# Attention tower: the softmax sums' reciprocals taken on 128 partitions, with two DMAs, in place of 64 partitions in slices

## The reference

```python
h = h + attn0(layernorm(h))      # 8 heads of 8 features, 1024 x 1024 scores, a window bias
h = h + ffn0(layernorm(h))       # two routed layers of 128, relu
h = h + attn1(layernorm(h))      # 8 heads of 8 features, no bias
h = h + ffn1(layernorm(h))       # 8 experts of 128, gelu, top 2
```

```python
attn = softmax(q @ k.T * 8 ** -0.5 (+ bias))   # over the last axis
out  = (attn @ v) @ proj_w.T + proj_b
```

## Time and profile before

| | us |
|---|---|
| median of 3 runs | 5202.08 |
| lowest, highest run | 5192.63, 5230.2 |
| the profiled execution | 5204.23 |
| its span | 5202.4 |

### The profile page before, as it was taken

How to read it: one execution, slowest core, us unless ns; L and a number is a source line. 1 busy time by engine, 2 the same in 40 slices (tenths; PEclk the granted TensorE clock), 3 DMA queues, 4 the chain that set the end, 5 groups by cost and what they waited for, 6 DMA issues and landing times.

```text
span 5202.4 us, 79603 instructions
## 1 busy us (share of the span) xinstructions
PE 4541.6 (87%) x21509; PEld 1547.7 (30%) x21509; DVE 3181.5 (61%) x5083; ACT 2836.1 (55%) x5086; POOL 800.6 (15%) x1198
## 2 busy tenths in 40 slices
PE   3787999998989989899898989989899898999696
PEld 2222333332333322233232333322233232332222
DVE  2565757666665766656566665766657566576561
ACT  0355656565655646565465655646566465666454
POOL 3102112011111111111011111211111011111100
PEclk8789999998998989998898999989899798999898
DMA  2213211212110121101212110121101212110100
GB/s 54 45 26 50 37 24 26 42 32 42 26 31 19 30 42 32 34 22 19 42 32 42 29 29 21 28 42 32 35 21 20 41 32 42 26 23 16 25 1 5
DMA packets 113100, 158.25 MB, mean 30 GB/s; under 512 B 18868, under 2 KB 60340, under 8 KB 112610
## 3 DMA queue, kind: packets, MB, share of 16 engines
q1 hardware_dynamic: 112646, 152.71, 16.3%
HBM read 120.36 MB, written 29.36 MB: 29 GB/s over the span
## 4 chain that ended last, share of the span: by engine, by line
PE 69%; DVE 10%; issue 10%; ACT 7%; DMA 2%; POOL 1%; SPq 0%; DVEq 0%; ACTq 0%; POOLq 0%
PE acc L818 18%; PE st L804 16%; PE nat L784 15%; DVE reciprocals L1108 4%; PE st L742 4%; DVE tile_max L1185 4%; ACT prob L986 3%; PE side L754 2%; PE side L649 2%; PE side L690 2%; DMA k_rows<-k_scratch 2%; PE side L664 1%; PE side L670 1%; PE side L709 1%; PE side L676 1%
## 5 line engine op out<-in xcount | busy, mean ns | idle before, releaser
L1185 DVE TENSOR_REDUCE tile_max<-nat 128x1 f32<-128x512 f32 x4096 | 2630.2, 685 | 1808.8 <-PE nat L784 1772.2
L986 ACT ACTIVATE prob<-st 128x512 f32<-128x512 f32 x4096 | 2299.6, 596 | 2122.0 <-PE st L804 2047.2
L784 PE MATMUL nat<-k_rows,q_rows 96*128 96x512 bf16 x4096 | 1648.8, 403 | 353.4 <-DVE tile_max L1185 149.2
L804 PE MATMUL st<-q_rows,k_rows 99*128 99x512 bf16 x4096 | 1641.1, 401 | 153.8 <-ACT prob L986 126.1
L818 PE MATMUL acc<-prob,v_padded 128*32 128x512 f32 x8192 | 1175.1, 648 | 1.0 <-ACT prob L986 1.0
L784 PEld LDWEIGHTS nat<-k_rows,q_rows 96*128 96x128 bf16 x4096 | 415.5, 101 | 1537.5 <-DVE tile_max L1185 1007.9
L804 PEld LDWEIGHTS st<-q_rows,k_rows 99*128 99x128 bf16 x4096 | 405.8, 99 | 992.5 <-ACT prob L986 704.2
L1328 POOL TENSOR_SCALAR max_parts<-neg_max 128x16 bf16<-128x16 f32 x128 | 26.4, 206 | 2274.5 <-DVE neg_max L1192 1764.4
L1108 DVE RECIPROCAL reciprocals<-side 64x128 f32<-64x128 f32 x256 | 244.6, 957 | 34.4 <-PE side L683 26.5
L818 PEld LDWEIGHTS acc<-prob,v_padded 128*32 128x32 f32 x8192 | 165.5, 111 | 333.1 <-issue 292.7
L742 PE MATMUL st<-ln_rows,w 128*128 128x512 f32 x512 | 242.7, 621 | 17.1 <-ACT hidden L959 12.6
(11 more groups left out here) (117 smaller groups left out, 2352.5 us busy)
## 6 DMA issues: line engine op xcount, KB each, us to landing
q_rows<-q_scratch SPq DMA_DIRECT2D x288, 128.0 KB
k_rows<-k_scratch SPq DMA_DIRECT2D x96, 384.0 KB
x_rows<-in_x SPq DMA_DIRECT2D x64, 512.0 KB, 6.7
q_scratch<-qk_parts SPq DMA_DIRECT2D x32, 384.0 KB
k_scratch<-qk_parts SPq DMA_DIRECT2D x96, 128.0 KB
group_weights<-in_routed SPq DMA_DIRECT2D x64, 129.0 KB, 2.1
q_rows<-max_rows SPq DMA_DIRECT2D x512, 3.0 KB
out_h<-out_rows SPq DMA_DIRECT2D x16, 256.0 KB, 2.0
```

Of the source, the lines that this page charges most:

```text
L784: eng.matmul(NAT[place % len(NAT)][:, :], QA[u][0:K_NAT, h, c:c + P], KA[u][0:K_NAT, h, kh * 512:kh * 512 + 512], start=True, stop=True)\
L804: eng.matmul(ST[n % 2][:, :], KA[u][0:K_ALL, h, t * P:t * P + P], QA[u][0:K_ALL, h, half * 512:half * 512 + 512], start=True, stop=True)\
L986: eng.activation(prob[:, n % TILES, :], ST[n % 2][:, :], ACT.Exp).then_inc(exp_done, 1)
L1185: eng.tensor_reduce(mx[:, q % 2, j // 8, j % 8 // 2, j % 2:j % 2 + 1], NAT[place % len(NAT)][:, :], AX.X, ALU.max).then_inc(nat_free, 1)
```

## The change

The reciprocal is taken before the heads are combined. Four rows of `acc_sb` (row 8 of each 32) hold all 8192 sums once. Stage `SR` (SP) moves them by one DMA of 32 KB to `sum_rows`, 128 partitions of 64 columns. `SI` (DVE) takes one reciprocal of 128 x 64. `SW` (SP) moves the result back into the four rows of `acc_sb`. `COMB` waits for that DMA and spreads the reciprocals in place of the sums. `CR` becomes two parts: ACT copies the bank's rows 64 to 127 to `reciprocal_rows` (64 x 512), and DVE multiplies. In the schedule `SR`, `SI`, `SW`, `COMB` and `CR` stand at tiles 4, 9, 10, 15, 16 (second attention) and at 131, 135, 136, 141, 142 (first attention); `PROJ` stays where it was.

```diff
@@ side_parts
-        n = 8 if name == "CR" else max(len(SIDE_BANKS.get(name, ())), 1)
+        n = 2 if name == "CR" else max(len(SIDE_BANKS.get(name, ())), 1)
@@ side_schedule, middle_of (called with n = 135)
-        for dn, name, *more in ((0, "COMB"), (1, "CR"), (13, "PROJ", 0), (15, "LN1", "a"),
+        for dn, name, *more in ((-4, "SR"), (0, "SI"), (1, "SW"), (6, "COMB"), (7, "CR"), (13, "PROJ", 0), (15, "LN1", "a"),
...
-            put(n + dn, name, b, *more, every={"COMB": 4, "CR": 1}.get(name, 2))
+            put(n + dn, name, b, *more, every=2)
@@ short_middle_of (n = 4 in pass 0, n = 137 in pass 14)
-        for dn, name, *more in ((0, "COMB"), (0, "CR"), (10, "PROJ", 0), (12, "LN1", "a"),
+        for dn, name, *more in ((-1, "SR"), (1, "SI"), (2, "SW"), (5, "COMB"), (6, "CR"), (10, "PROJ", 0), (12, "LN1", "a"),
@@ the second attention's tail
-        put(9, "COMB", r - 1, every=4)
-        put(10, "CR", r - 1, every=1)
+        put(4, "SR", r - 1)
+        put(9, "SI", r - 1)
+        put(10, "SW", r - 1)
+        put(15, "COMB", r - 1)
+        put(16, "CR", r - 1)
         put(22, "PROJ", r - 1, 1)
@@ tiles
-        rec = sb("reciprocals", [64, 512])
+        sums = sb("sum_rows", [P, 64])
+        rec = sb("reciprocals", [P, 64])
+        rrow = sb("reciprocal_rows", [64, 2, 512])
@@ SyncE
+                elif name in ("SR", "SW"):
+                    rows = acc_sb[HD::32, :, :]
+                    if name == "SR":
+                        alone(eng.wait_ge(acc_free, at(N_ACC * (n["SR"] + 1))))
+                        eng.dma_start(sums[:, :], rows).then_inc(sum_in, 16)
+                    else:
+                        alone(eng.wait_ge(rec_ready, at(n["SW"] + 1)))
+                        eng.dma_start(rows, rec[:, :]).then_inc(rec_in, 16)
@@ TensorE, COMB
-                    eng.wait_ge(acc_free, at(N_ACC * (n["COMB"] + 1)))
+                    eng.wait_ge(rec_in, at(16 * (n["COMB"] + 1)))
@@ ScalarE
+                elif name == "CR":
+                    eng.wait_ge(side_full[k], at(n[f"bank{k}"]))
+                    eng.wait_ge(tail_d, at(2 * n["CR"]))
+                    eng.activation(rrow[:, k, :], SIDE[k][64:P, :], ACT.Copy).then_inc(rrow_ready, 1)
@@ VectorE, CR
-                    bank, c = k // 4, k % 4 * P
-                    before = 4 * n["CR"] + 2 * bank
-                    eng.wait_ge(side_full[bank], at(n[f"bank{bank}"]))
-                    if c == 0:
+                    eng.wait_ge(rrow_ready, at(2 * n["CR"] + k + 1))
+                    if k == 0:
                         eng.wait_ge(hres, at(n["CR"]))
-                        eng.wait_ge(tail_d, at(before))
-                    ins = eng.reciprocal(rec[:, c:c + P], SIDE[bank][64:P, c:c + P])
-                    if k % 4 == 3:
-                        ins.then_inc(tail_d, 1)
-                        eng.wait_ge(tail_d, at(before + 1))
-                        eng.tensor_tensor(OT[0:64, bank * 512:bank * 512 + 512], SIDE[bank][0:64, :],
-                                          rec[:, :], ALU.mult).then_inc(side_free[bank], 1)
-                        eng.wait_ge(side_free[bank], at(n[f"bank{bank}"]))
-                        eng.sem_inc(tail_d, 1)
+                    eng.tensor_tensor(OT[0:64, k * 512:k * 512 + 512], SIDE[k][0:64, :],
+                                      rrow[:, k, :], ALU.mult).then_inc(side_free[k], 1)
+                    eng.wait_ge(side_free[k], at(n[f"bank{k}"]))
+                    eng.sem_inc(tail_d, 1)
+                elif name == "SI":
+                    eng.wait_ge(sum_in, at(16 * (n["SI"] + 1)))
+                    eng.wait_ge(rec_in, at(16 * n["SI"]))
+                    eng.reciprocal(rec[:, :], sums[:, :]).then_inc(rec_ready, 1)
```

More of the change, by code:

```diff
@@ L270 @@
 NAMES = ["LX", "TOKA", "TOKB", "TOKC", "LN1", "LN2", "TR", "QK", "QV", "SCR", "VC", "RL", "HO0", "HO1",
-         "COMB", "CR", "ZK", "PROJ", "BO", "H1", "L0", "L1", "WO", "GATE", "RANK", "MT", "OUT", "WCL", "WCA",
+         "SR", "SI", "SW", "COMB", "CR", "ZK", "PROJ", "BO", "H1", "L0", "L1", "WO", "GATE", "RANK", "MT", "OUT", "WCL", "WCA",
          "bank0", "bank1", "FWA", "FWB"] + [f"FY{k}" for k in range(E + 1)]
@@ L411, in tower_kernel @@
         tail_d, hres = sem("tail_d"), sem("hres")
+        sum_in, rec_ready, rec_in = sem("sum_in"), sem("rec_ready"), sem("rec_in")
+        rrow_ready = sem("rrow_ready")
         bo_done, hid_ready, wc_in, wc_ready = sem("bo_done"), sem("hid_ready"), sem("wc_in"), sem("wc_ready")
@@ L686, in side_stage @@
                 elif name == "PROJ":
-                    eng.wait_ge(tail_d, at(4 * (n["PROJ"] + 1)))
+                    eng.wait_ge(tail_d, at(2 * (n["PROJ"] + 1)))
                     bk = side_bank(n, 0)
@@ L967, in acc_out @@
                 if q % SUPERS == 0:
-                    eng.wait_ge(tail_d, at(4 * (over(n0, ATTN) + q // SUPERS)))
+                    eng.wait_ge(tail_d, at(2 * (over(n0, ATTN) + q // SUPERS)))
                 eng.wait_ge(pv_done, at(n0 + SUPER * (q + 1)))
```

## The result

The changed kernel takes 5311.5 us (median of 4 runs, 5292.7 to 5325.0) against 5216.1 us for the kernel before (4 runs, 5192.6 to 5230.2): ratio 1.0185, 95% interval 1.0127 to 1.0243. It is slower by 1.85%, about 95 us. The forecast was 5220 us, 0.3% slower. The profiled execution took 5304.0 us, its span 5302.2 us.

The account below looks back on a forecast made before the run. PE bounds on average, DVE locally at the reciprocals. Terms -158 - 8 - 15 + 176 + 22 = +17 on 5204.2 us give 5221, as a median 5220 against 5202; range 5130 to 5310.

Parts of the forecast that it names:

- Second tails: Second attention's tail, tiles 8 to 24, fifteen times: without the DVE reciprocals 10.5 us less each, 158 us less.
- First tails of passes 1 to 13: First attention's tail, tiles 131 to 152: SR lands with RL, DVE and PE stall; +13.5 us each, +176 us.
- the third rival: Tiles 139 to 152 of thirteen passes: clock stays slow through COMB and PROJ, 4.7 us more per pass, 5295 us; chance 0.24.
- Pass 0: Tail with RL at tile 136, ahead of SW: COMB on PE waits for RL, tile 152 comes 22 us later.
- The short tails: Pass 0's first attention and pass 14's, no RL near: gain 7 or 8 us each, 15 us less.
- RL no longer beside the loop edge: Pass start, tile 0: PE's instruction wait may be shorter without RL's traffic; 8 us less in all (0 to 20).
- The row maxima of tile 23: Their DMAs queue behind the second attention's RL, needed at tile 32: 0 to 2 us lost each, taken as 0.
- the relief didn't outweigh the stall: Rival, both attentions' tails: second tails gain 12.4 us, stalls cost 10.5, 5145 us in all; chance 0.16.
- SR was held up: First tails: SR lands with RL, 24 us after issue. Rival that it isn't held up: 4918 us, chance 0.06.
- the slower case: Whole kernel slower by over 1%: chance 0.28, of which 0.24 was for slow clock at tiles 139 to 152.
- its rival's 0.96: New reciprocal on DVE, taken at 0.48 us: rival says up to 0.96 us, about 5235 us; chance 0.02.
- The ring order of one queue: SP's queue, first tails: DMA engines take descriptors in ring order, so SR lands 24 us after issue, not 2.

Follow-up runs that it names:

- e2: Changed kernel with the second attention's reload RL at tile 32 in place of 16: 5218.6 us, ratio 1.0012 to the kernel before.
- e3: Changed kernel with RL at tile 32 (second attention) and at 152 (first attention): 4891.9 us, ratio 0.9381 to the kernel before.
- e4: Kernel before, with its own reciprocals, and RL moved to tiles 32 and 152: 5212.2 us, ratio 0.9983.
- e6: Changed kernel with SR and SW issued by ScalarE on its own DMA queue, RL left in place: 5325.4 us, ratio 1.0236 to the kernel before.
- e8: Changed kernel with the first attention's RL at tile 137, directly behind SW; second attention's stays at 16: 5076.8 us, ratio 0.9727 to the kernel before.
- e1: Changed kernel with the first attention's RL at tile 152 in place of 130 and 136: 4991.6 us, ratio 0.9591 to the kernel before.
- e5: Changed kernel without SR, SI and SW, rows multiplied by the sums, so part of the computation is left out: 4889.4 us, ratio 0.9401 to the kernel before.

## Why the prediction was wrong

The sign of the measured difference was that of the forecast, its size wasn't: +18 us expected, +95 measured, and 5311.5 lies just outside the range. Step by step:

- *Second tails.* Expected -158, measured -161 (the table's -153.5 without the -3.9 of pass 0's short tail, and the last phase's -10.9). Right: tiles 8 to 24 take 18.3 us at clock 1.00 in nearly every pass. PROJ came down to 62.5 / 32 = 2.0 us, the value taken from `w_v`'s row.
- *First tails of passes 1 to 13.* Expected +176, measured 575.3 - 403.5 = +172. Right, with the mechanism as far as the waits go: SR behind RL, DVE in order behind SI, PE behind three nat banks. For pass 5, 13.4 more were expected and 12.1 came (42.8 against 30.7). The slow clock behind the pause lasted about as long as the earlier trace rows had it: 0.62 on average from 2121.5 to 2126, then 1.00. So the third rival, slow clock through COMB and PROJ, didn't happen.
- *Pass 0.* Expected +22, measured 54.5 - 31.8 = +22.7.
- *The short tails.* Expected -15, measured -6.5 in pass 14 and -3.9 in pass 0: 5 us off.
- *RL no longer beside the loop edge.* Expected -8, measured +8.8 for tiles 0 to 8. The instruction waits there didn't shrink: PE's nat matmuls waited 102.2 us for issue, against 101.7. RL's traffic was not what made them long. The runs with RL at 32 (e2, e3, e4) have 184.6 to 193.1 us for these tiles, so the +8.8 are within what these tiles vary by.
- *The row maxima of tile 23.* This is the step that failed: "It comes out with 0 to 3 us to spare; 0 to 2 us lost each, I take 0." Measured +71 us, and e2 shows that it is due to RL in front of them. The mechanism was named, and tile 32 waiting for `max_rows` was among the signs of being wrong; the size taken was too small. PE without the wait is at tile 32 29.4 us after tile 9 (e2, mean of passes 1 to 13), inside what was worked out. But RL starts 2.2 us after tile 9 in most passes and not 1.5, and its last data packet comes 25.1 to 31.6 us after its first issue, 28.7 on average, not 26; the maxima land behind that. So PE waited for them in each of passes 1 to 14, 0.2 to 7.8 us, 63.6 in all. A margin of 0 to 3 us is none when the transfer's length spreads over six. PE's clock drops with the waits (0.69 from 1957 to 1968), which fits the 7 us that remain.

With +71 in place of 0 and the loop edge at 0, the same sum (-158 - 15 + 176 + 22 + 71 = +96) gives 5300 on the old base of 5204.2, and the profiled execution took 5304.0. Of the rivals, the relief didn't outweigh the stall, SR was held up as expected, and the time came out in the slower case (chance 0.28) by a mechanism that was none of the rivals, though it stood among the terms. The new reciprocal took 0.55 us, not the 0.48 taken, far from its rival's 0.96.

On one point the reason given was too simple. The ring order of one queue was said to be what holds SR up; the `x_edge` row it rested on can't tell order from traffic, since those loads were issued right behind the large ones on the same queue. e6 shows that most of the delay remains on a queue of its own. The Trainium skill's "DMA: Bandwidth & Descriptors", Why a DMA increments its semaphore by 16 and not by 1, which the prediction cites, would put SR on four engines that also carry RL; e6 agrees with that (17.6 us on an otherwise empty queue). The number four shows in the traces: SR's completion comes as five signals, in pass 5 of e6 one 1.1 us after the issue and four at 17.5 to 17.6 us. Which engines these are isn't shown, nor the share of each, so it remains an explanation and not a finding.

Why RL is slower at tiles 12 to 40 (28.7 us) than at tiles 0 to 17 (24.7 us on average) wasn't tried either. The trace shows one thing that may add to it: in passes 3 to 13 of the changed kernel LX's two 512 KB loads are issued 27.8 us after tile 9 (1958.43 in pass 5), before RL and the maxima have landed, and the DMA share from 1957 to 1968 is 0.92. Before, RL had landed long before they were issued. It can't be all: in pass 14, which has no such load there, RL takes 25.7 us to its last completion signal in the changed kernel but 30.9 in e8. No run moved LX.

## What to carry to other kernels

A small DMA that an in-order engine waits for must be placed by what is in flight when it is issued, not by its own 2 us: list every transfer that is issued ahead of it, and move the bulk load, not the small one, into a stretch where no small one is due within its length. Here the same edit is worth -6% or +1.9%, by two numbers in the schedule. And where a deferred bulk load gets in front of another small transfer with a margin no wider than the load's own spread, count the late cases; an early one gives nothing back.

## What the runs showed of the hardware

- A 32 KB DMA between SBUF tiles took 18.8 us on average on ACT's own queue while 2.36 MB were under way on SP's (e6), 24.1 behind them on SP's (the changed kernel), and 2.3 with nothing large under way (e1).
- The same twelve loads, 2.36 MB, took 22.6 to 31.6 us from the first issue to the last data packet (passes 1 to 14 of the kernel before, the changed one, e1 and e2).
- A reciprocal of 128 x 64 from SBUF took 548 ns on DVE; half of the 957 for twice the columns would be 479.
- Taking the reciprocals (245 us of busy time) from DVE took some 320 us from the whole when nothing else stood in the way (e5): a stretch in which another engine held PE back cost twice, in the wait and in the 1.2 GHz behind it.
